# Two heads' sums ahead of the spread of the maximum on TensorE (graph attention layer of a four-layer GNN)

## The reference, cut to what matters

```python
z = jnp.einsum('nd,hdf->nhf', h, W)
es = jnp.einsum('nhf,hf->nh', z, a_src)
ed = jnp.einsum('nhf,hf->nh', z, a_dst)
e = jax.nn.leaky_relu(es[src] + ed[dst], SLOPE)
e = jnp.where(e == 0.0, NEG, e)
m = jax.ops.segment_max(e, dst, num_segments=N)
...
ex = jnp.exp(e - m[dst])
denom = jax.ops.segment_sum(ex, dst, num_segments=N)
...
alpha = ex / safe
out = jax.ops.segment_sum(alpha[:, :, None] * z[src], dst, num_segments=N)
```

## Time and profile before

| | us |
|---|---|
| median of 3 runs | 1993.73 |
| lowest, highest | 1992.58, 1993.85 |
| profiled execution | 1987.39 |
| its span, first to last instruction | 1985.6 |

### The profile page before, as it was taken

The page is one execution under the profiler, slowest core; times in us unless marked ns, Lnnn a source line. Parts: engine busy times, 40 slices in busy tenths (PEclk is TensorE's granted clock), DMA queues, the critical chain, the costliest instruction groups (busy, mean ns, idle before and its releaser), DMA issues.

```text
span 1985.6 us, 37417 instructions
## 1 busy us (share of the span) xinstructions
PE 1685.3 (85%) x13647; PEld 1458.5 (73%) x13647; DVE 1245.3 (63%) x2739; ACT 448.6 (23%) x996; POOL 645.0 (32%) x539
## 2 busy tenths in 40 slices
PE   5568999899998999997388888887888887899998
PEld 4347777777776888886277777777777775788887
DVE  8568989889896111222488887788888788321211
ACT  0242232322221000102132233332233325200000
POOL 0034443455452000001455555555555530000000
PEclk9889999999999999998556555556555567999999
DMA  7902212122124344441233333333333322244441
GB/s 124 111 11 103 103 71 103 71 103 100 74 104 197 113 145 144 144 145 58 76 85 88 88 88 88 88 85 88 88 88 88 88 57 100 105 153 169 170 152 45
DMA packets 75841, 203.58 MB, mean 103 GB/s; under 512 B 37259, under 2 KB 51951, under 8 KB 66063
## 3 DMA queue, kind: packets, MB, share of 16 engines
q1 hardware_dynamic: 54671, 141.84, 22.2%
q0 software_dynamic: 20992, 59.37, 11.4%
HBM read 152.90 MB, written 53.57 MB: 104 GB/s over the span
## 4 chain that ended last, share of the span: by engine, by line
PE 69%; DVE 13%; issue 7%; SPq 3%; another core or an unknown queue 3%; ACT 2%; DVEq 1%; DMA 1%; ACTq 0%
PE bank L1219 27%; PE bank L1287 13%; PE bank L1163 10%; PE bank L1268 5%; PE bank L1155 4%; PE bank L1277 3%; PE bank L1181 2%; SPq L321 2%; PE bank L1152 2%; DVE big L806 2%; DVE work L979 1%; DVE work L960 1%; PE bank L1227 1%; DVE x_sb L817 1%
## 5 line engine op out<-in xcount | busy, mean ns | idle before, releaser
L462 POOL DMA_INDIRECT ring<-attention_rows,work x420 | 398.5, 949 | 304.8 <-remote 161.3
L1287 PE MATMUL bank<-work,ring 128*65 128x48 f32 x3360 | 382.6, 299 | 0.0
L1287 PEld LDWEIGHTS bank<-work,ring 128*65 128x65 f32 x3360 | 368.3, 220 | 1.8
L1219 PE MATMUL bank<-big,ring 128*128 128x256 f32 x1250 | 273.0, 379 | 1.4 <-DVE x_sb L832 1.4
L1219 PE MATMUL bank<-big 128*128 128x256 f32 x1250 | 272.9, 379 | 0.0
L1219 PEld LDWEIGHTS bank<-big,ring 128*128 128x128 f32 x1250 | 236.5, 190 | 33.8 <-DVE x_sb L832 2.2
L1219 PEld LDWEIGHTS bank<-big 128*128 128x128 f32 x1250 | 236.6, 190 | 31.7
L1163 PE MATMUL bank<-big 128*128 128x256 bf16 x1875 | 209.0, 273 | 14.6 <-ACT big L505 14.6
L1163 PEld LDWEIGHTS bank<-big 128*128 128x128 bf16 x1875 | 181.4, 98 | 39.0 <-ACT big L505 18.3
L1277 PE MATMUL bank<-ident,work 96*128 96x96 f32 x336 | 86.0, 402 | 116.0 <-DVE work L960 113.4
L1152 PE MATMUL bank<-work 128*128 128x100 bf16 x800 | 153.3, 211 | 21.9 <-DVE big L806 14.2
(11 more groups left out here) (211 smaller groups left out, 2065.2 us busy)
## 6 DMA issues: line engine op xcount, KB each, us to landing
adjacency<-big SPq DMA_DIRECT2D x25, 1600.0 KB, 5.2
ring<-adjacency SPq DMA_DIRECT2D x25, 1600.0 KB, 7.2
big<-adjacency SPq DMA_DIRECT2D x25, 1600.0 KB, 7.3
ring<-attention_rows,work POOLq DMA_INDIRECT x420
edge_rows<-edge_list SPq DMA_DIRECT2D x1, 4983.0 KB
x_sb<-in_x SPq DMA_DIRECT2D x1, 3072.0 KB
out_x<-xnT SPq DMA_DIRECT2D x24, 128.0 KB, 4.3
attention_rows<-ring SPq DMA_DIRECT2D x13, 135.0 KB, 2.3
```

The lines of the kernel that those rows point to most:

```text
L462: G.indirect_dma_start(out=rows[0:EP, s, c, 0:ZG], out_offset=None, in_=ztab[:, :], in_offset=bass.IndirectOffsetOnAxis(ap=idx[:, g, c:c + ...
L1219: ins = mm(bank[:, 0:D], slots[s][:, b, :], ybuf[:, b, :], start=(b == 0), stop=(b == NT - 1))
L1287: ins = mm(sum_banks[k % 3][0:FH, h * WIN:(h + 1) * WIN], rows[0:EP, s, c, h * FH:(h + 1) * FH], prob[:, k % 2, c, h * WIN:(h + 1) * WIN], ...
```

## The change

In PE's list of layer 2 the sums of heads 0 and 1 of the former group are issued between transpose_hots(g+2) and spread_max(g); those of heads 2 and 3 stay behind destination_logits(g+2). Before, head 0 stood behind spread_max(g) and heads 1 to 3 behind destination_logits(g+2). The instructions and their waits are the same.

```diff
@@ -1294,14 +1294,14 @@
                         transpose_max(g)
                     if has(g + 2):
                         transpose_hots(g + 2)
+                    if has(g - 1):
+                        sums(g - 1, range(0, 2))
                     if has(g):
                         spread_max(g)
-                    if has(g - 1):
-                        sums(g - 1, range(0, 1))
                     if has(g + 2):
                         destination_logits(g + 2)
                     if has(g - 1):
-                        sums(g - 1, range(1, H))
+                        sums(g - 1, range(2, H))
```

## The result

| | before | after |
|---|---|---|
| median, us | 1993.15 | 2100.82 |
| lowest, highest | 1991.22, 1993.85 | 2100.11, 2102.30 |
| profiled execution, its span | 1987.39, 1985.6 | 2100.11, 2098.3 |
| layer 2, first gather to last addition | 937.3 to 1643.7 = 706.4 | 931.0 to 1755.8 = 824.8 |

Four runs of each: the kernel is 107.7 us slower, a ratio of 1.0543 (95% interval 1.0525 to 1.0561). The forecast was slower, 2053 us, with a range to 2112: right in its sign, short by 48 us of 108. In the two profiled executions all of it lies in layer 2, which is 118.4 us longer in that of after and began 6.3 us earlier there: 118.4 - 6.3 = 112.1, and the spans differ by 112.7.

What follows compares the result with a forecast made beforehand. The bound was taken as a loop of PE's late completions and POOL's five gathers, 8.05 us a group. 80 x (8.70 - 8.05) = 52 us plus 7 of (e) gave 59, 2046.4 profiled, 2053 us as median; range 2006 to 2112.

Steps and rivals of the forecast that it cites:

- (a): PE ahead of the spread: its idle 1.39 us a group can take the moved sums, 2.2 us at the low clock.
- (d): End of PE's group: later slot_free from the last sums and the wait for the banks' former contents, both free.
- (b): New loop from new_max through the exponential, 20 sums and spread: 8.30 us a group against 8.05, 20 us over 80 groups.
- (c): Spread's completion behind 20 sums with gathers in flight: late by 0 to 1.1 us, taken as 0.4, so 8.70 a group.
- R2: Spread's completion held to the end of the gather burst: 9.4 us a group, 2109 us; chance 0.20.
- R1: Only the loop of (b), spread's completion not late: 8.30 us a group, 2021 us; chance 0.24.
- R4: No change, the gather loop of 8.05 us sets the pace: 1993.7 us, within 4; chance 0.08.
- R3: TensorE's clock at 2.4 GHz shortens the loop to 6.8 us; with half the stage at either clock, 1954 us; chance 0.08.
- (e): Four groups without gathers at the stage's ends: 8.3 us instead of 6.5, 4 x 1.8 = 7 us.

Runs made afterwards that it cites:

- one gather: From the sixth group on only one of the five columns is gathered: before's order 1891.67 us, after's order 2007.90 us.
- the run without the wait: After's order, but the 20 sums ahead of the spread read another tile and don't wait for prob_ready: 2040.17 us beside 1991.18 of before.
- one head ahead: Against before, only head 0's 10 sums moved ahead of the spread: 1992.93 us beside 1997.34; again, 1986.05 beside 1992.93, ratio 0.9968.
- all heads ahead: Against before, all 40 sums moved ahead of the spread, none behind: 2199.72 us.
- short rows: From the sixth group on the five gathers fetch 18 numbers per row instead of 270: before's order 1989.78 us, after's order 2101.56 us.
- x_sb: After's order, but the sums' weight loads read another tile instead of the ring that the gathers write: 2102.54 us.
- sixteen ahead: Against before, 16 sums (head 0 and three columns of head 1) moved ahead of the spread, 24 behind the logits: 2100.36 us.
- two heads behind the spread: Against before, head 1's sums moved ahead of the logits product, the spread left ahead of all sums: 1997.63 us beside 1992.93.

## Why the prediction was right in sign and 48 us short

**What bounds the kernel before** was right. The 1.2 us by which L960 was late were read as the gathers' doing; with one gather they are gone and the kernel is 101 us faster. That the clock has no part in the lateness held too: in before, from 1100 to 1500 us, L960 starts 2.27 to 2.37 us behind the burst's last gather in all 50 groups, whether the spread takes 1.17 us or 0.68.

**(a)** held: PE's gap ahead of the spread closed. **(d)**, the last sums' later completion, was put at nothing; no run tests it by itself.

**(b), the loop**, held within 0.05 us: 8.30 predicted, 8.35 measured with one gather at the clock of 0.50. Its cost with one gather, 116 us, is that of 80 groups by 8.35 - 6.9 = 1.45. The gap of PE ahead of the sums was predicted as 1.4 and is 1.31.

**(c), the lateness of the spread's completion**, is the mis-sized term: 0.4 us predicted, 1.1 measured, the upper end of its bounds. In the two groups shown the spread is seen 1.66 and 0.83 us behind its end, instead of 0.14; less that, 1.52 and 0.69, mean 1.1, as over all groups from 1100 to 1500 us (1.27 - 0.14). With the loop: 8.35 + 1.52 = 9.87 and 8.35 + 0.69 = 9.04, and the groups measured 9.85 and 9.03 (L969 from 1307.26 to 1316.29 is the second). The sum with 1.1 in its place is 80 x (8.30 + 1.1 - 8.05) + 7 = 115 us, against 118.4 in layer 2. The step that failed was "20 sums are nearer to the ten than to the 40". It took the lateness for a quantity that grows with the sums ahead. The runs with 10, 16, 20 and 40 ahead show no such growth: not held, held, held to the same point, not held. So rival R2, given 0.20, was right in mechanism and nearly in size (9.4 us, 2109 us), and the forecast's own middle was a compromise between two states of which neither lies there. That 2101 us stands inside the range is owed to R2's bound and not to the forecast's own sum.

**R1** (loop alone) is what the trace shows at the end of the layer and with one gather, and only there. **R4** fell with the first row of L969. **R3**, the clock, went the other way: PE had no less waiting, the gap only moved, and the granted clock stayed at 0.50, that is 1.2 GHz, with PE busy 573.1 of 741 us (77%) instead of 525.6 of 641 (82%) at 0.57. Its sum for the loop was sound all the same: 6.8 us, and 6.85 measured with one gather where the clock was 0.74. The Trainium skill (TensorE: Matmul & The Clock Gate, Part 1: The HAM clock gate) has activity lift the clock; these two traces agree in direction, for the change made PE less busy. But busy time alone doesn't account for it: the run without the wait has PE busy 329.9 of 400 us (1100 to 1500) at 0.50, before 327.6 at 0.57. Why the clock fell stays open.

**(e)** took 8.3 - 6.5 = 1.8 us for each of four groups without gathers. At the end of the layer it is 8.03 - 6.5 = 1.5, so 6 us instead of 7 if the two at the start, which weren't measured, are alike.

## What to carry to other kernels

When an instruction that others wait for is moved behind work with a wait of its own, draw the loop through both and add it up; the filled gap says nothing if it is the same wait, moved. A lateness seen on one instruction goes to whichever takes its place in the same burst; count how much of the work ahead of it runs inside the burst, and price the lateness by where the burst ends, not by interpolating over the work in the list. Where a cost has two states, let the forecast be one of them. And say at which clock a loop is priced: this one was 8.35 us at 1.2 GHz and 6.85 in a stretch at a higher clock.

## What the runs showed of the hardware

While POOL issues a burst of five indirect gathers, a completion of TensorE can reach its waiter long behind the recorded end of the instruction: mostly 2.0 to 2.5 us behind the start of the burst's last gather. Before, after and every experiment with five gathers show it, but the one with all 40 sums ahead. Where no burst runs, it is 0.03 to 0.4 us behind PE's end. It concerns DVE and SP as waiters alike.

A burst alone doesn't do it; it goes with the sums that PE has run inside the burst before the completion. The logits product L1259 and the load L379 that waits for it show this best. Counted from 1100 to 1500 us, a sum being inside the burst when it starts behind the start of the burst's first gather:

| sums run inside the burst ahead of L1259 | kernels | L379 starts behind the end of L1259 by | and beside the start of the burst's last gather |
|---|---|---|---|
| none | one head ahead (both runs), all heads ahead | 0.17 to 0.20 us | in mid-burst |
| about 10 | before, with full and with short rows | 0.18 to 1.9 us | 2.0 to 2.8 us ahead of it |
| 16 or 20 | after, after with short rows, with x_sb, without the wait, sixteen ahead | 0.3 to 2.1 us | 2.2 to 2.5 us behind it |
| 20 | two heads behind the spread | 2.4 to 5.5 us | 0.8 to 2.4 us behind it |

Turns with no sums in flight bear it out: in after L1268 (1309.42 to 1310.08) runs in a burst, and L960 finds it complete at 1311.40, in mid-burst. The lateness depends on how many gathers there are, not on their bytes (74 or 6 GB/s), nor on the tile that the sums' weight loads read, nor on the clock. PE's ends in these profiles are modelled, so that the sums themselves end later than their records inside a burst is a rival that no run tells from a semaphore that comes late.

The Trainium skill (DMA: Bandwidth & Descriptors, section SWDGE vs HWDGE vs iDMA) says that for such a transfer POOL's cores compute a pair of descriptors for every DMA operation and append it to rings in SBUF. The short rows left POOL's 0.95 us a gather as it was, which fits that part of the work as the cause. It doesn't show it: no run here counts the descriptors (the packets of POOL's queue fell from 20992 to 14672), nor how they would hold back a completion. The same skill's page SBUF — State Buffer (section SBUF: two separate sides), by which the engines' ports and the DMA's can't contend and PE never waits on anyone there, isn't contradicted as to the ports, for the bytes don't matter. But a reader who takes (c) as nothing by it is 1.1 us a group short, and the measurement decides.

Three things stay open: what inside the chip holds the completion, why sums inside the burst are needed for it, and why the kernel without the wait settles with its 20 sums inside a burst while the one with one head ahead keeps its ten outside.
